# Attention, routing and 32 experts on one core: output rows by rank, experts from last to first, weights kept whole

## The chip, the cores and the metric

The kernel runs on 1 core of one Trainium2 chip. The metric is the device time in microseconds of one execution. The trace is of one profiled execution on the same kind of core.

## What is computed

A time-mixing attention over 8 batches of 128 positions and 256 channels, a residual sum, and then a mixture of experts: each of the 1024 tokens picks 4 of 32 experts, each expert takes at most 256 tokens, and a shared expert is added. All is float32. Cut to what matters:

```python
def wkv(time_decay, time_first, k, v):            # per channel, over t
    w, u = -exp(time_decay), time_first
    y_t = (exp(pp - q) * aa + exp(u + k_t - q) * v_t) / (exp(pp - q) * bb + exp(u + k_t - q))
    ...
x  = x + wkv(td, tf, layernorm(x), ctx)
z  = rmsnorm(layernorm(x)) * norm_w               # 1024 tokens x 256
scores  = softmax(z @ gate_w.T)                   # 32 experts
w, ids  = top_k(scores, 4);  w = w / sum(w)
buf[expert, position in expert] = z[token]        # 32 x 256 slots, further ones dropped
act = silu(buf @ w13[:, :128]) * (buf @ w13[:, 128:])
routed[token] += (act @ w2)[expert, position] * w
out = x + layernorm(x) + routed + (silu(z @ sg) * (z @ su)) @ sd
```

## The kernel before

**Queues.** Five engines run their own programs and meet by semaphores. SyncE (SP) issues nearly all plain transfers in the order of its program; GpSimd (POOL) issues the indirect ones, which scatter 128 rows each by a list of row numbers; ScalarE (ACT) stores three output tiles.

**Attention and routing** (`run`, lags of stages over the 8 batches). DVE, ACT and PE work a batch through scan, reciprocal, residual sum and norms to the normed rows `n_row`. For each batch DVE finds the 4 best logits (`top_logits`, `top_experts`, L632 and L636), writes the expert numbers plus one into `tags` (`expert_tags`, L640), and makes a one-hot, a mask and with TensorE's counts the slot of each pick (`slot_numbers`, L666). ACT makes the weights' exponentials per batch (`negative_max`, `pick_weights`, L450 and L454) and copies the tags beside the rows (`tag_rows`, L459). GpSimd scatters each batch's rows four times, once for each pick, into `rows_in` (`scatter`, L318), which has 1024 rows for each expert and was zeroed by 32 transfers of SyncE (L204).

**Between.** ACT takes the silu of the shared expert (L470), DVE multiplies (L675), and PE runs the shared down matmuls (L859), then eight matmuls whose result isn't used (L864), and then the experts. SyncE has issued four loads of expert weights `w13b` of 256 KB (L210) and four of `w2_all` of 1 MB (L227) after the zeroing, waits for all scatters, and loads the rows of the first four experts.

**Experts**, from 0 to 31, in this order for each engine:

- PE: transposes of the next expert's rows (`rows_to_channels`, L874), gate and up matmuls of this one (`gate_up`, L882), down matmul of the one before (`down`, L899). The slots are in two halves of 128. The second half is worked only if the expert has more than 128 rows: PE loads a flag from `big` (`value_load`) and branches. In float32 each matmul with weights stands in the trace as two records.
- ACT: `rows_to_sbuf` (copy of the next rows to `xT`, two instructions, L476), `silu` (L481).
- DVE: `picks_of_slots` (finds the output row of each slot, three small operations, L718 to L724), `gated` (product, L730), `rows_out_to_sbuf` (copy of the result to `yo`, L737).
- GpSimd: `scatter_out`, two scatters of 128 rows to `rows_out`, to the row 4 x token + pick (L333). Slots without a pick are out of bounds and write nothing.
- SyncE: `refill`: rows of the expert four ahead, weights three ahead, and one row to `last_rows` for the overflow case (L214, L210, L221).

`w13b`, the rows `xg`, `yo` and `pick_idx` are rings of four (`WB`). The first four experts are written out; the ones from 4 to 27 run in loops (`Fori`) of four experts an iteration on SyncE, ACT and DVE; on GpSimd all 32 do. In a loop a wait compares a semaphore with a number worked out from the loop's counter. PE's program is written out whole. If an expert has more than 256 picks, GpSimd mends rows under a flag.

**Tail.** When all scatters have landed, SyncE loads `G` tile by tile, each with its four picks (L265). DVE sums five tiles, weighting by `w_all` (L769). ACT weights the other three (L503) and GpSimd adds them (L372).

## Time and profile before

| | us |
|---|---|
| median of 3 runs | 234.11 |
| the runs | 232.91 to 234.96 |
| span of the profiled execution | 228.0 |
| first transpose of the experts | 82.08 |
| last scatter of output rows starts | 200.99 |

The profile gives for each engine its busy time and for each group of instructions the source line, what it writes and reads, and what its engine waited for before it. PE is TensorE's matmuls, PEld its weight loads, DVE VectorE, ACT ScalarE, POOL GpSimd, SPq SyncE issuing transfers. "issue" and "remote" are waits whose releaser the profile doesn't show.

### The profile page before, as it was taken

What the parts mean: (1) busy time and instruction counts of PE and PEld (TensorE: products, weight loads), DVE (VectorE), ACT (ScalarE), POOL (GpSimd) and SP (SyncE); (2) the same over time, 40 slices, a digit from 0 to 9 for tenths busy, and PEclk for the clock granted to TensorE, in tenths of its full rate; (3) what the DMA queues carried; (4) which work ended last, traced back from release to release, by engine and by line L of the source; (5) the groups of instructions that cost most, each with busy time, mean ns of one, the idle gap of its engine ahead of it and who ended that gap; (6) DMA issues with size and microseconds to landing.
All of it is one profiled execution on the core that took longest, in us unless ns stands there. A gap on an engine that the chain in (4) does not pass through costs nothing.

```text
span 228.0 us, 3659 instructions
## 1 busy us (share of the span) xinstructions
PE 139.5 (61%) x819; PEld 119.8 (53%) x819; DVE 120.4 (53%) x385; ACT 84.8 (37%) x254; POOL 115.6 (51%) x140
## 2 busy tenths in 40 slices
PE   1124887787774879969895948858499479200000
PEld 0112765676663559959794837837398377100000
DVE  2878999997433344555253531536237055303990
ACT  3165678566563024434214231335225032002410
POOL 6201156888877500754563736555464646632740
PEclk9999996555555799988999788999979958755555
DMA  5999999998222264775775657465665731129930
GB/s 173 334 340 340 338 339 364 365 373 301 96 99 95 95 198 134 235 204 153 218 198 176 192 161 220 136 189 158 185 172 171 232 115 52 43 69 359 385 122 23
DMA packets 40270, 46.46 MB, mean 204 GB/s; under 512 B 4585, under 2 KB 37045, under 8 KB 40252
## 3 DMA queue, kind: packets, MB, share of 16 engines
q1 hardware_dynamic: 35200, 37.30, 53.2%
q0 software_dynamic: 4608, 8.54, 10.5%
q10 hardware_dynamic: 444, 0.40, 0.5%
q8 instruction: 9, 0.15, 0.2%
q14 instruction: 9, 0.07, 0.1%
HBM read 27.95 MB, written 22.45 MB: 221 GB/s over the span
## 4 chain that ended last, share of the span: by engine, by line
PE 36%; issue 20%; SPq 19%; another core or an unknown queue 7%; DVE 7%; DMA 5%; ACT 2%; POOL 0%; POOLq 0%; ACTq 0%; DVEq 0%
PE bank L882 18%; PE bank L899 11%; SPq L204 10%; PE bank L874 8%; SPq L227 5%; DVE part L769 4%; DMA G<-rows_out 3%; DVE act_t L730 1%; ACT xT L476 1%; DMA xg<-rows_in 1%; ACT sg L481 1%; DVE res L769 1%; SPq L210 1%; DMA rows_out<-yo,pick_idx 1%
## 5 line engine op out<-in xcount | busy, mean ns | idle before, releaser
L333 POOL DMA_INDIRECT rows_out<-yo,pick_idx x64 | 62.6, 978 | 55.7 <-issue 47.8
L882 PE MATMUL bank<-xT,w13b 128*128 128x128 f32 x368 | 51.6, 294 | 8.5 <-issue 5.6
L882 PEld LDWEIGHTS bank<-xT,w13b 128*128 128x128 f32 x368 | 48.1, 208 | 11.0 <-issue 11.0
L476 ACT ACTIVATE xT<-bank,cols 128x256 f32<-128x256 f32 x64 | 26.8, 473 | 43.0 <-PE bank L874 37.0
L899 PE MATMUL bank<-w_all,act_t 128*128 128x256 f32 x92 | 29.7, 434 | 16.0 <-DVE act_t L730 14.9
L730 DVE TENSOR_TENSOR act_t<-sg,bank 128x256 f32<-128x256 f32 x32 | 13.5, 421 | 49.3 <-ACT sg L481 36.5
L318 POOL DMA_INDIRECT rows_in<-n_row,slot_all x32 | 32.5, 1015 | 10.0 <-issue 10.0
L481 ACT ACTIVATE sg<-bank 128x256 f32<-128x256 f32 x32 | 12.3, 386 | 44.6 <-PE bank L882 25.1
L899 PEld LDWEIGHTS bank<-w_all,act_t 128*128 128x128 f32 x92 | 16.5, 209 | 18.8 <-issue 17.9
L737 DVE COPY yo<-bank 128x512 f32<-128x512 f32 x32 | 22.0, 687 | 6.6 <-remote 3.3
L874 PE MATMUL bank<-ident,xg 128*128 128x128 f32 x128 | 22.0, 301 | 1.3 <-DMA xg<-rows_in 1.2
L874 PEld LDWEIGHTS bank<-ident,xg 128*128 128x128 f32 x128 | 18.0, 157 | 6.2 <-issue 2.7
L839 PE MATMUL bank<-hT,sgu 128*128 128x128 f32 x64 | 16.1, 432 | 0.0
L308 POOL TENSOR_TENSOR rs<-ve,neg_half 128x2 f32<-128x2 f32 x8 | 5.9, 736 | 17.4 <-DVE ve L624 17.3
L839 PEld LDWEIGHTS bank<-hT,sgu 128*128 128x128 f32 x64 | 14.3, 326 | 0.0
L503 ACT ACTIVATE G<-G,w_all 128x256 f32<-128x256 f32 x12 | 5.1, 496 | 17.1 <-DMA G<-rows_out 17.1
L810 PE MATMUL bank<-ident,n_row 128*128 128x128 f32 x16 | 5.3, 430 | 9.6 <-ACT n_row L431 9.6
L718 DVE SCALAR_TENSOR_TENSOR own<-xg,iota_e 128x8 f32<-128x8 f32 x32 | 7.0, 219 | 7.4 <-issue 4.4
L562 DVE TENSOR_TENSOR_SCAN S<-decay,bank 128x512 f32<-128x512 f32 x8 | 9.7, 1209 | 1.1 <-PE bank L794 1.1
L769 DVE SCALAR_TENSOR_TENSOR part<-G,w_all,base_all 128x256 f32<-128x256 f32 x5 | 3.8, 767 | 10.4 <-DMA G<-rows_out 10.4
L794 PE MATMUL bank<-ident,ek 128*128 128x128 f32 x16 | 5.1, 420 | 6.4 <-DVE ekv L556 6.3
L819 PE MATMUL bank<-gwT,hT 128*128 128x32 f32 x32 | 7.5, 374 | 1.8 <-ACT hT L444 1.8
(109 smaller groups left out, 194.3 us busy)
## 6 DMA issues: line engine op xcount, KB each, us to landing
rows_in<-zeros SPq DMA_DIRECT2D x32, 264.0 KB, 6.4
xg<-rows_in SPq DMA_DIRECT2D x32, 264.0 KB
w13b<-in_L_ffn_w_dram SPq DMA_DIRECT2D x32, 256.0 KB
w_all<-in_L_ffn_w_dram SPq DMA_DIRECT2D x4, 1024.0 KB
...
rows_out<-yo,pick_idx POOLq DMA_INDIRECT x64
...
```

The costliest lines, as they stand in the source:

```text
L204: sp.dma_start(zv[a * P:(a + 1) * P, e:e + 2, :], zeros[:, 0:2 * RW].rearrange("p (e c) -> p e c", e=2)).then_inc(zeroed[a], 16)
L318: pool.indirect_dma_start(rows_in, bass.IndirectOffsetOnAxis(ap=slot_all[:, b, k:k + 1], axis=0), n_row[:, b, :], None)\
L333: pool.indirect_dma_start(rows_out, bass.IndirectOffsetOnAxis(ap=pick_idx[:, q, a:a + 1], axis=0), yo[:, q, a, :], None, bounds_check=PICK ...
L476: act.activation(xT[:, j, h, :], FX[j][:, h, :], ACT.Copy, scale=nw[:, h:h + 1]).then_inc(s["f_x"], 1)
L481: act.activation(sg[:, j, :], FG[j][:, 0, :], ACT.Silu).then_inc(s["f_s"], 1)
L730: dve.tensor_tensor(act_t[:, j, :], sg[:, j, :], FG[j][:, 1, :], ALU.mult).then_inc(s["f_a"], 1)
L737: dve.tensor_copy(yo[:, q, :, :], FY[q % 2]).then_inc(s["f_yo"], 1)
L769: dve.scalar_tensor_tensor(out=dst, in0=G[:, b, k, :], scalar=w_all[:, b, k:k + 1], in1=src, op0=ALU.mult, op1=ALU.add)\
L839: last = nc.tensor.matmul(SGU[:, a, :], sgu[:, h, a, :], hT[:, j, h, :], start=(h == 0), stop=(h == HC - 1))
L874: last = nc.tensor.transpose(FX[q % 2][:, h, a * P:(a + 1) * P], xg[q][:, a, h * P:(h + 1) * P], ident[:, :])
L882: last = nc.tensor.matmul(FG[q % 2][:, a, cols], w13b[q][:, h, a, :], xT[:, q % 2, h, cols], start=(h == 0), stop=(h == HC - 1))
L899: return nc.tensor.matmul(FY[q % 2][:, a, :], act_t[:, q % 2, a * P:(a + 1) * P], w2_all[:, bass.ds(e, 1), :].rearrange("p o c -> p (o c)" ...
```

## The change

- **Order of picks.** `picks_in_order` copies the 4 expert numbers beside 4 negative pick numbers and takes the 8 largest: experts in falling order, then pick numbers. These lie in `n_row` itself, so the scatter carries them; `tags` and ACT's copy are gone. Rank 0 is the token's highest expert. Row numbers of the output are 1024 x rank + token, from the highest rank block down.
- **Weights.** The exponentials are made once for all batches: DVE subtracts (`expo`), ACT exponentiates before the shared silu, and `weights_in_order`, on DVE after the third expert, sums, divides and sorts them into the new order.
- **Experts run from 31 to 0**, all programs written out, waits against constants. After 29 of them every token's rank 0 has been written, after 30 rank 1, after 31 rank 2 (`settles`).
- **Weights whole in SBUF.** `w13_all` holds all experts. Five 1 MB loads of it and three of `w2_all` are issued before the row loads, the other four during the first experts. An expert's result `yo` overwrites its own `w13` weights, and `G` the weights of four finished experts. Rings of `yo` and `pick_idx` and the waits on them are gone; the rows' ring has 6 buffers. `last_rows` is stored by two transfers.
- **Halves.** A full expert runs 4 gate and up matmuls of 256 columns, not 8 of 128. The 32 flags are bits of two numbers (`bit`, `halves`), loaded once by PE.
- **Tail.** `G` is loaded rank by rank, 1 MB each with rows of 1 KB; the last rank in four pieces. DVE sums tiles 0 to 3 in place. PE sums tiles 4 to 7 in PSUM: the base through the identity, each rank through a diagonal of its weights, made by ACT in `weight_diagonal` during the experts. ACT copies and stores these. GpSimd sums nothing.

```diff
-POOL_SUMS = (1, 3, 6)
+SUMS_DVE = B // 2
+SETTLED = E - K + 1
+DIAG_FROM = 6
 FIRST = 2
 W2L = 4
+W13L = 8
+EARLY = 5
+XB = 6
+AHEAD = 2
+BITS = 16
...
+        w13_all = sb("w13_all", [P, E, HC, 2, F])
         w2_all = sb("w2_all", [P, E, C])
-        xg = [sb(f"xg{q}", [P, 2, RW]) for q in range(WB)]
-        own = sb("own", [P, WB, 2, K])
-        owned = sb("owned", [P, WB, 2])
-        pick_idx = sb("pick_idx", [P, WB, 2], I32)
+        xg = [sb(f"xg{q}", [P, 2, RW]) for q in range(XB)]
+        own = sb("own", [P, E, 2, K])
...
+        yo = [w13_all[:, e].rearrange("p h a f -> p (h a f)").rearrange("p (a c) -> p a c", a=2) for e in range(E)]
+        G = [w13_all[:, E - 4 * (k + 1):E - 4 * k].rearrange("p e h a f -> p (e h a f)").rearrange("p (b c) -> p b c", b=B)
+             for k in range(K)]
+        total = x_all
+        diag = v_all[:, :, :].rearrange("p b c -> p (b c)").rearrange("p (q r c) -> p q r c", q=B - SUMS_DVE, r=K)
...
+            def load_w13(g):
+                sp.dma_start(w13_all[:, E - (g + 1) * n:E - g * n].rearrange("p e h a f -> p (e h) (a f)"),
+                             w13[E - (g + 1) * n:E - g * n].rearrange("e (h p) f -> p (e h) f", p=P)).then_inc(w13_in[g], 16)
+
+            def load_w2(g):
+                sp.dma_start(w2_all[:, E - (g + 1) * m:E - g * m, :],
+                             w2[E - (g + 1) * m:E - g * m].rearrange("e p c -> p e c"))\
+                    .then_inc(w2_in[g], 16)
...
+            for g in range(EARLY):
+                load_w13(g)
+                if g % 2 == 0:
+                    load_w2(g // 2)
...
+            for i in range(XB):
+                load_rows(i)
+            for i in range(E):
+                if i + XB < E:
+                    sp.wait_ge(s["f_xt"], i + 1)
+                    sp.wait_ge(s["own_done"], i + 1)
+                    load_rows(i + XB)
+                if i % 2 == 0 and EARLY + i // 2 < W13L:
+                    load_w13(EARLY + i // 2)
+                    if (EARLY + i // 2) % 2 == 0:
+                        load_w2((EARLY + i // 2) // 2)
+                if i == E // 2 + 2:
+                    sp.wait_ge(s["f_yo"], E // 2)
+                    store_last(0)
+
...
+            ranked = rows_out.rearrange("(r n) c -> r n c", r=K)
+            for r in range(K):
+                sp.wait_ge(row_out[r], 32 * SETTLED if r == 0 else 32)
+                if r == 0:
+                    sp.wait_ge(s["f_yo"], E)
+                    store_last(1)
+                    sp.wait_ge(s["fixed"], fixes)
+                rows = ranked[K - 1 - r].rearrange("(h b p) c -> p h b c", h=2, p=P)
+                home = G[r].rearrange("p (h b) c -> p h b c", h=2)
+                if r < K - 1:
+                    sp.dma_start(G[r], ranked[K - 1 - r].rearrange("(b p) c -> p b c", p=P)).then_inc(gathered[r], 16)
+                else:
+                    for c in range(SUMS_DVE):
+                        sp.dma_start(home[:, :, c, :], rows[:, :, c, :]).then_inc(last_gathered[c], 16)
...
+            pool.memset(bit[:, :], 1.0).then_inc(s["bit_set"], 1)
+            for i in range(4):
+                odd = bit[:, :].rearrange("p (g o n) -> p g o n", o=2, n=1 << i)[:, :, 1, :]
+                pool.wait_ge(s["bit_set"], i + 1)
+                pool.tensor_scalar(odd, odd, float(1 << (1 << i)), None, ALU.mult).then_inc(s["bit_set"], 1)
...
-            def scatter_out(e, q):
-                pool.wait_ge(s["pick_ready"], e + 1)
-                pool.wait_ge(s["f_yo"], e + 1)
-                pool.sem_inc(s["held_pool"], 1)
+            def scatter_out(i, e):
+                pool.wait_ge(s["f_yo"], i + 1)
                 for a in range(2):
-                    pool.indirect_dma_start(rows_out, bass.IndirectOffsetOnAxis(ap=pick_idx[:, q, a:a + 1], axis=0),
-                                            yo[:, q, a, :], None, bounds_check=PICKS - 1, oob_is_err=False)\
-                        .then_inc(row_out[q], 16)
-
+                    pool.indirect_dma_start(rows_out, bass.IndirectOffsetOnAxis(ap=pick_idx[:, e, a:a + 1], axis=0),
+                                            yo[e][:, a, :], None, bounds_check=PICKS - 1, oob_is_err=False)\
+                        .then_inc(row_out[settles(i)], 16)
...
+            act.wait_ge(s["expo_done"], 1)
+            act.activation(ew[:, :, :], expo[:, :, :], ACT.Exp).then_inc(s["ew_ready"], 1)
...
+            def weight_diagonal(q):
+                b, r = SUMS_DVE + q // K, q % K
+                if q == 0:
+                    act.wait_ge(s["w_done"], 1)
+                act.activation(diag[:, q // K, r, :], ident[:, :], ACT.Copy, scale=w_all[:, b, r:r + 1])\
+                    .then_inc(s["diag_done"], 1)
...
+            for q in range(B - SUMS_DVE):
+                act.wait_ge(s["tile_summed"], q + 1)
+                act.activation(total[:, q, :], FT[q], ACT.Copy).then_inc(s["tile_ready"], 1)
+                act.wait_ge(s["tile_ready"], q + 1)
+                act.dma_start(ov[:, SUMS_DVE + q:SUMS_DVE + q + 1, :], total[:, q:q + 1, :]).then_inc(act_out_done, 16)
...
-            def expert_tags(b, j):
+                dve.max_index(idx8[:, b, :], top8[:, b, :], LG).then_inc(s["idx_done"], 1)
+
+            def picks_in_order(b, j):
                 dve.wait_ge(s["idx_done"], b + 1)
-                dve.tensor_scalar(tags[:, b, 0:K], idx8[:, j, 0:K], 1.0, None, ALU.add).then_inc(s["expert_ready"], 1)
+                if b == 0:
+                    dve.wait_ge(s["pickno_ready"], 1)
+                dve.tensor_copy(picks[:, b, 0, :], idx8[:, b, 0:K]).then_inc(s["picks_copied"], 1)
+                dve.wait_ge(s["picks_copied"], b + 1)
+                dve.max(n_row[:, b, TAG:RW], picks[:, b].rearrange("p g k -> p (g k)")).then_inc(s["expert_ready"], 1)
...
+            dve.tensor_tensor(expo[:, :, :], top8[:, :, 0:K], top8[:, :, 0:1].to_broadcast([P, B, K]), ALU.subtract)\
+                .then_inc(s["expo_done"], 1)
...
+            def weights_in_order():
+                dve.wait_ge(s["ew_ready"], 1)
+                dve.tensor_reduce(esum[:, :], ew[:, :, :], AX.X, ALU.add).then_inc(s["esum_done"], 1)
+                dve.tensor_tensor(same[:, :, :, :], n_row[:, :, TAG:TAG + K].unsqueeze(3).to_broadcast([P, B, K, K]),
+                                  picks[:, :, 0, :].unsqueeze(2).to_broadcast([P, B, K, K]), ALU.is_equal)\
+                    .then_inc(s["same_done"], 1)
+                dve.wait_ge(s["esum_done"], 1)
+                dve.reciprocal(rsum[:, :], esum[:, :]).then_inc(s["rsum_done"], 1)
+                dve.wait_ge(s["rsum_done"], 1)
+                dve.tensor_tensor(w_pick[:, :, :], ew[:, :, :], rsum[:, :].unsqueeze(2).to_broadcast([P, B, K]), ALU.mult)\
+                    .then_inc(s["w_pick_done"], 1)
+                dve.wait_ge(s["same_done"], 1)
+                dve.wait_ge(s["w_pick_done"], 1)
+                dve.tensor_tensor(same_w[:, :, :, :], same[:, :, :, :],
+                                  w_pick[:, :, :].unsqueeze(2).to_broadcast([P, B, K, K]), ALU.mult)\
+                    .then_inc(s["same_w_done"], 1)
+                dve.wait_ge(s["same_w_done"], 1)
+                dve.tensor_reduce(w_all[:, :, :], same_w[:, :, :, :], AX.X, ALU.add).then_inc(s["w_done"], 1)
...
+            for e in range(AHEAD):
+                picks_of_slots(e)
+            for e in range(E):
                 gated(e, e % 2)
                 if e:
-                    rows_out_to_sbuf(e - 1, e - 1, 0)
-            with dve.Fori(1, E // WB - 1) as i:
-                for q in range(WB):
-                    picks_of_slots(WB * i + q, q, i)
-                    gated(WB * i + q, q % 2)
-                    rows_out_to_sbuf(WB * i + q - 1, (q - 1) % WB, i - (q == 0))
-            for e in range(E - WB, E):
-                picks_of_slots(e, e % WB, e // WB)
-                gated(e, e % 2)
-                rows_out_to_sbuf(e - 1, (e - 1) % WB, (e - 1) // WB)
-            rows_out_to_sbuf(E - 1, WB - 1, E // WB - 1)
-
-
-            dve.wait_ge(s["sh_b"], B // 2)
-            dve.wait_ge(s["w_done"], 1)
-
-            mine = [b for b in range(B) if b not in POOL_SUMS]
-            for n, b in enumerate(mine):
-                dve.wait_ge(gathered[b], 16)
-                for k in range(K):
-                    src = base_all[:, b, :] if k == 0 else part[:, n % 2, k - 1, :]
-                    dst = res[:, b, :] if k == K - 1 else part[:, n % 2, k, :]
-                    if k:
-                        dve.wait_ge(s["tail_part"], (K - 1) * n + k)
-                    if b == B - 1 and k == K // 2:
-                        dve.wait_ge(gathered[B], 16)
-                    dve.scalar_tensor_tensor(out=dst, in0=G[:, b, k, :], scalar=w_all[:, b, k:k + 1], in1=src,
-                                             op0=ALU.mult, op1=ALU.add)\
-                        .then_inc(s["res_ready" if k == K - 1 else "tail_part"], 1)
+                    rows_out_to_sbuf(e - 1)
+                if e + AHEAD < E:
+                    picks_of_slots(e + AHEAD)
+                if e == 2:
+                    weights_in_order()
...
+            for r in range(K):
+                if r < K - 1:
+                    dve.wait_ge(gathered[r], 16)
+                for b in range(SUMS_DVE):
+                    if r == K - 1:
+                        dve.wait_ge(last_gathered[b], 16)
+                    if r:
+                        dve.wait_ge(s["tail_part"], (r - 1) * SUMS_DVE + b + 1)
+                    dve.scalar_tensor_tensor(out=base_all[:, b, :], in0=G[r][:, b, :], scalar=w_all[:, b, r:r + 1],
+                                             in1=base_all[:, b, :], op0=ALU.mult, op1=ALU.add)\
+                        .then_inc(s["res_ready" if r == K - 1 else "tail_part"], 1)
...
-            def gate_up_half(q, a, cols):
-                for h in range(HC):
-                    last = nc.tensor.matmul(FG[q % 2][:, a, cols], w13b[q][:, h, a, :], xT[:, q % 2, h, cols],
-                                            start=(h == 0), stop=(h == HC - 1))
-                return last
-
-            def gate_up(e, q, n, second):
-                pe.wait_ge(w_in[q], 16 * (n + 1))
-                pe.wait_ge(s["f_x"], 2 * e + 2)
-                if not isinstance(e, int) or e >= 2:
-                    pe.wait_ge(s["f_a"], e - 1)
+            def gate_up_slots(e, j, slots):
+                for a in range(2):
+                    for h in range(HC):
+                        last = nc.tensor.matmul(FG[j][:, a, 0:slots], w13_all[:, expert(e), h, a, :], xT[:, j, h, 0:slots],
+                                                start=(h == 0), stop=(h == HC - 1))
+                last.then_inc(s["f_g"], 1)
...
+            flags = [pe.value_load(big[0:1, g:g + 1], min_val=0, max_val=(1 << BITS) - 1) for g in range(E // BITS)]
+
+            def second(e):
+                return flags[expert(e) // BITS] & (1 << expert(e) % BITS)
...
+            pe.wait_ge(s["sh_b"], B // 2)
+            pe.wait_ge(s["diag_done"], (B - SUMS_DVE) * K)
+            for q in range(B - SUMS_DVE):
+                nc.tensor.matmul(FT[q], ident[:, :], base_all[:, SUMS_DVE + q, :], start=True, stop=False)
+            for r in range(K):
+                if r < K - 1:
+                    pe.wait_ge(gathered[r], 16)
+                for q in range(B - SUMS_DVE):
+                    if r == K - 1:
+                        pe.wait_ge(last_gathered[q], 16)
+                    last = nc.tensor.matmul(FT[q], diag[:, q, r, :], G[r][:, SUMS_DVE + q, :], start=False,
+                                            stop=(r == K - 1))
+                    if r == K - 1:
+                        last.then_inc(s["tile_summed"], 1)
```

## Rows read from the trace of the kernel before

**Rows 1.** Table by stages: stretch, length; PE, PEld, DVE, ACT, POOL busy; clock; DMA; GB/s.

```profile
20.00:30.00 10.00, 7.31 (x32) 5.95 (x32) 9.22 (x31) 7.85 (x27) 0.70 (x1) 1.00 1.10 339
82.00:198.20 116.20, 90.75 (x588) 80.18 (x588) 49.01 (x161) 37.28 (x96) 60.03 (x62) 0.90 0.57 168
198.20:228.00 29.80, 0.00 (x0) 0.00 (x0) 13.45 (x20) 5.12 (x12) 11.74 (x15) 0.50 0.51 187
```

**Rows 2.** Timeline before the experts: start, length, engine, line, what, idle before.

```profile
31.48 1.31 POOL L318 DMA_INDIRECT rows_in<-n_row,slot_all  x1 [0.28 <-issue]
...
33.94 11.90 SPq L227 DMA_DIRECT2D w_all<-in_L_ffn_w_dram  x4
...
76.65 0.96 POOL L318 DMA_INDIRECT rows_in<-n_row,slot_all  x1 [0.30 <-issue]
```

**Rows 3.** Chain that ended last, first experts: start, us, what.

```profile
86.35 1.79 PE bank L882 x16
88.14 0.87 PE bank L899 x4
89.00 0.44 PE bank L874 x4
...
94.72 0.89 PE bank L882 x8
```

**Rows 4.** Groups of instructions: busy us, mean ns, idle before.

```profile
L899 PE MATMUL bank<-w_all,act_t 128*128 128x256 f32 x92 | 29.7, 434 | 16.0 <-DVE act_t L730 14.9 <-issue 1.2
```

**Rows 5.** Timeline in the experts.

```profile
90.64 1.20 POOL L333 DMA_INDIRECT rows_out<-yo,pick_idx  x1 [6.95 <-DVE pick_idx L724]
...
157.46 1.13 PE L882 MATMUL bank<-xT,w13b 128*128 128x128 f32 x8
...
159.39 0.98 POOL L333 DMA_INDIRECT rows_out<-yo,pick_idx  x1 [0.30 <-issue]
...
160.67 0.97 POOL L333 DMA_INDIRECT rows_out<-yo,pick_idx  x1 [0.30 <-issue]
...
161.59 0.23 DVE L718 SCALAR_TENSOR_TENSOR own<-xg,iota_e 128x8 f32<-128x8 f32 x1 [3.36 <-issue]
...
164.02 0.00 SPq L214 DMA_DIRECT2D xg<-rows_in  x1
...
164.11 0.39 ACT L481 ACTIVATE sg<-bank 128x256 f32<-128x256 f32 x1 [4.90 <-remote]
```

**Rows 6.** Waits: engine, line, releaser: us in total, times, longest.

```profile
ACT sg L481 <- remote: 18.2, 5, 5.7
```

**Rows 7.** Timeline of the last expert and the tail.

```profile
194.87 0.38 ACT L481 ACTIVATE sg<-bank 128x256 f32<-128x256 f32 x1 [3.28 <-remote]
...
203.44 4.89 SPq L265 DMA_DIRECT2D G<-rows_out  x9
206.78 0.48 DVE L769 SCALAR_TENSOR_TENSOR part<-G,w_all,base_all 128x256 f32<-128x256 f32 x1 [8.58 <-DMA G<-rows_out]
...
222.11 0.48 DVE L769 SCALAR_TENSOR_TENSOR res<-G,w_all,part 128x256 f32<-128x256 f32 x1
```

**Rows 8.** The same chain at the last scatter.

```profile
200.99 2.30 DMA rows_out<-yo,pick_idx
```

**Rows 9.** Timeline of the shared expert and the first transposes.

```profile
68.10 1.28 ACT L470 ACT_TABLE_LOAD   x1
69.39 1.06 ACT L470 ACTIVATE sg_all<-gu_all 128x1024 f32<-128x1024 f32 x1
70.02 0.29 DVE L666 TENSOR_REDUCE slot_all<-picked 128x4 int32<-128x128 f32 x1
70.48 1.23 DVE L675 TENSOR_TENSOR sg_all<-sg_all,gu_all 128x1024 f32<-128x1024 f32 x1 [0.17 <-issue]
...
82.08 1.30 PE L874 MATMUL bank<-ident,xg 128*128 128x128 f32 x8 [1.19 <-DMA xg<-rows_in]
```

**Rows 10.** DMA traffic in GB/s in 40 slices of 5.7 us.

```profile
GB/s 173 334 340 340 338 339 364 365 373 301 96 99 95 95 198 134 235 204 153 218 198 176 192 161 220 136 189 158 185 172 171 232 115 52 43 69 359 385 122 23
```

311 lines of the change are left out of this document (118 added, 193 removed).

## The prediction, made before the changed kernel was run

> **What bounds the kernel now.** I read the table by stages first [rows 1]: attention and routing up to 82 us, the 32 experts from 82 to 198.2 us, then the tail to 228.0 us. No engine is full in the experts: TensorE 0.78 of the time, GpSimd 0.52.
>
> In the first part GpSimd issues 32 scatters of input rows, from 31.48 to 76.65, one each 1.46 us, and the last comes with no wait but its issue [rows 2]. That stream sets the end.
>
> In the experts the chain of work gives TensorE's price [rows 3]. A full expert (over 128 slots) takes 0.44 + 1.79 + 0.87 = 3.10 us (86.35 on), a half one 0.44 + 0.89 + 0.43 (half of the 0.87) = 1.76. The down matmuls are 92 records, two per matmul [rows 4]: 46 matmuls for 32 experts, so 14 are full. TensorE needs 14 x 3.10 + 18 x 1.76 = 75.1 us of the 116.1 us (82.1 to 198.2); 41.0 are lost. GpSimd's output scatters come 1.28 us apart [rows 5]: 64 x 1.28 = 81.9, also less than 116.1.
>
> Where the 41 us lie is the main point. In [rows 5] an expert's up matmuls start at 157.46 and take 1.13 us, but ScalarE's silu of them starts at 164.11, after 4.90 us idle put down to "remote". SyncE's row load of 164.02 comes at that moment too, although the VectorE work it waits for ended at 161.82. So signals come late, on several engines at once. The waits [rows 6] hold 18.2 us of this on the silu line alone. In this stage SyncE, ScalarE, VectorE and GpSimd run in loops (`Fori`) and wait against computed numbers. While three of them were still in written-out code, TensorE ran without a gap [rows 3]. But the last silu, written out too, idles 3.28 us on "remote" [rows 7], so loops may not be the whole cause.
>
> The tail: the last scatter starts at 200.99 and lands 2.30 later [rows 8], SyncE starts the `G` loads at 203.44, VectorE's last sum ends at 222.6, and 5.4 us of output and closing follow [rows 7].
>
> **The change, part by part.** The profiled span is 228.0 us and the median of the runs 234.11; I keep the 6.1 between them.
>
> *Start.* `picks_in_order` puts a COPY and a MAX8 where one TENSOR_SCALAR stood. At this size I bound both by 0.29 from above (the 0.29 of [rows 9] works on 128 columns) and by nothing from below, and take 0.2 more a batch. VectorE is full there (9.22 of 10 us [rows 1]), for two batches before GpSimd's stream is closed: +0.4, scatters end at about 78. Four ScalarE operations a batch go; ScalarE had room (7.85 of 10), so nothing is gained. Five small operations for `bit` go to GpSimd when it is nearly idle (0.70 of 10). SyncE issues eight 1 MB loads ahead of the row loads where it had four and four small ones. Four took 11.90 us, so from 33.94 eight take it to 58 [rows 2]; its next work is at 78. The 3 MB more fill 9 us of the DMA after 57 us, where it moves only 96 GB/s [rows 10].
>
> ScalarE's Exp and the silu behind it now wait for `expo`, and so for VectorE's last slot numbers. These end at 70.31; + 0.2 (subtract) + 0.3 (Exp) + 1.28 + 1.06 (table, silu) + 1.23 makes 74.6 for `sg_all`, where it was 71.71 [rows 9]. The shared matmuls, the warming ones and the first transposes follow in TensorE's order. TensorE waited 1.19 us for the row loads [rows 9], which covers 1.1 of these 2.9: +1.8, the first transpose at 83.9. The flags' `value_load`, now two ahead of the experts, is not shown: 0 to 0.5, hidden by the warming matmuls.
>
> *Experts.* Full experts run four up matmuls of 256 columns, eight records at 0.87/4 = 1.73, not 1.79: TensorE 14 x 3.04 + 18 x 1.76 = 74.3. Waits on rings go, and nothing is queued behind GpSimd, since `yo` lies in each expert's own weights. VectorE works 49.0/32 = 1.53 us an expert [rows 1], under 1.76. `weights_in_order`, seven operations of 0.2 to 0.3, adds 1.5 once; the 16 diagonals are at most 0.39 each on ScalarE (the silu of twice the columns [rows 5]), which works 37.3/32 = 1.2 an expert. GpSimd's stream hides all of it: 81.9 against 74.3. Without that cover the 1.5 costs 1.5. The order turned round puts a full expert first and a half one second, 0.9 better for the first `yo`, + 1.8: the first scatter goes from 90.64 [rows 5] to 91.5, the last starts 63 x 1.28 later, at 172.1, against 200.99.
>
> *Tail.* The first rank waits for 29 experts: 172.1 - 7.7 + 2.3 = 166.7, then `store_last`, 0.3. It also waits for the last `yo`, which TensorE leaves at about 160. 512 KB land 3.3 us after the issue (203.44 to 206.78) and as much again at 385 GB/s [rows 10] takes 1.4: some 4.6 for 1 MB, then one each 2.6 to 3.1 us; I take 2.9. Ranks land at 171.6, 174.5, 177.4, the four pieces of the last (issued 174.5 to 176.3) by 180.3. VectorE adds four tiles a rank at 0.48 (the rate at 222.11), hidden. TensorE does four matmuls a rank, two records each: 0.43 a matmul at the higher clock, 0.86 at the lower, and it starts at the lower, as the tail of before shows 0.50 [rows 1]. All low it ends at 185.3, all high at 180.7. It had come up during the shared matmuls; I take 181.0. Copy 0.5, handing over 0.4, then 5.4: 187.3.
>
> A word on run length. Rank loads move 1 KB runs where 4 KB were read. The slices show 338 to 373 GB/s with 1 KB runs at the start, 359 and 385 in the tail [rows 10]; hence the 2.6 to 3.1. The Trainium skill ("Perfetto Trace Analysis", DMA Optimizations) says that DMAs under 2 KB have a significant overhead each. It gives no figure to put in the sum; the slices here show under a tenth.
>
> *Sum.* Last scatter 28.9 earlier, tail 27.0 to 15.2: 228.0 - 28.9 - 11.8 = 187.3; + 6.1 = 193.4. I say 194.
>
> **The rivals.** *Half the lateness stays (204 us).* Part of the 41.0 us isn't the loops': TensorE ends at 83.9 + 74.3 + 20.5 = 178.7, the last scatter starts 2.8 later (198.2 to 200.99 before), 9.4 after the forecast's; one more for less overlap. For it: the last silu. The Trainium skill ("Advanced Engine Details and Errata", ISA Cache) says that an engine other than TensorE holds 32 KB of instructions, 512 of them, so written-out loops must be fetched as they run. No row here shows a wait for that.
>
> *All of it stays (226 us).* It belongs to the output scatters, not the loops. TensorE ends at 83.9 + 74.3 + 41.0 = 199.2; rank loads start only then, the first lands at 204.2, the last at 212.9; + 7.0 + 6.1 = 226.0. For it: the stall of [rows 5] lasts as long as GpSimd issues. Against it: GpSimd streamed from 31 to 78 us too, and the others kept its pace.
>
> *Slower (261 us).* The same mechanism, but GpSimd is no longer held to four experts, streams without end, and TensorE's signals pass only when it rests. They take turns: 83.9 + 74.3 + 81.9 = 240.1, + 15 + 6. It decides from 49 us of lateness on, against 41.0 now. Against it: GpSimd issued for 82 us, and half of that was lost.
>
> **How the numbers follow.** Forecast 0.50, half 0.24, all 0.19, slower 0.04, something within 1% 0.03. A measurement of this kernel can't tell 1% from no change. Faster: 0.93. The floor is 194 less the start's 1.8, less 1.2 (2.6 a rank) and some 2 us of the 6.1 and the tail: 189; I go to 188. The upper end takes in the half case and half of the next: 222. The forecast's own range is 188 to 199, with the slow TensorE tail at its top.
>
> **What would show it.** Right: output scatters 1.28 us apart without gaps, TensorE's experts done some 8 to 10 us before GpSimd's, silus within 0.5 us of their matmuls, first transpose near 83.9, ranks landing 2.6 to 3.1 us apart. Wrong: GpSimd idle between experts, "remote" waits on the silu line, or rank loads that begin only after the last scatter. The forecast fails most easily at the 41 us, which I give to the loops on thin evidence.

## The result, and the profile after

| | before | after |
|---|---|---|
| median, 5 runs each | 232.91 us | 218.10 us |
| the runs | 232.23 to 234.96 | 215.86 to 218.78 |
| ratio | | 0.936 (0.930 to 0.942) |
| span of the profiled execution | 228.0 | 214.1 |
| first transpose of the experts | 82.08 | 90.89 |
| TensorE's last down matmul ends | 197.46 | 191.19 |
| last output scatter starts | 200.99 | 196.75 |

Faster, by 14.8 us where I forecast 40. The 13.9 us between the spans are made up of a loss of 8.8 at the start, a gain of 15.1 in the experts (115.4 to 100.3 on TensorE) and one of 7.6 behind TensorE's last down matmul (30.5 to 22.9).

The start first. GpSimd's timeline of the changed kernel (start, length, engine, line, what, idle before):

```profile
2.08 0.10 POOL L305 MEMSET var_add<- 128x1 f32 x1
11.31 0.16 POOL L306 IOTA iota_e<- 128x32 f32 x1 [9.13 <-issue]
...
40.38 1.31 POOL L342 DMA_INDIRECT rows_in<-n_row,slot_all  x1 [0.21 <-issue]
...
84.74 0.96 POOL L342 DMA_INDIRECT rows_in<-n_row,slot_all  x1 [0.30 <-issue]
```

GpSimd stands still for 9.13 us before its first index tile, waiting for nothing that the profile shows. In the kernel before, the input scatters ran from 31.48 to 76.65 [rows 2]; here all of them are 8 to 9 us later. I had nothing of this in the sum.

The experts, timeline and waits of the changed kernel:

```profile
90.89 1.04 PE L870 MATMUL bank<-ident,xg 128*128 128x128 f32 x8
...
98.58 1.20 POOL L355 DMA_INDIRECT rows_out<-w_all,pick_idx  x1 [6.51 <-DVE w_all L744]
...
103.44 1.06 PE L879 MATMUL bank<-xT,w_all 128*128 128x128 f32 x8
...
105.97 1.06 PE L879 MATMUL bank<-xT,w_all 128*128 128x128 f32 x8
...
107.77 0.97 POOL L355 DMA_INDIRECT rows_out<-w_all,pick_idx  x1 [0.30 <-issue]
109.36 0.38 ACT L477 ACTIVATE sg<-bank 128x256 f32<-128x256 f32 x1 [4.17 <-remote]
110.11 0.68 DVE L744 COPY w_all<-bank 128x512 f32<-128x512 f32 x1
...
111.57 0.97 POOL L355 DMA_INDIRECT rows_out<-w_all,pick_idx  x1 [2.83 <-DVE w_all L744]
```

```profile
POOL rows_out L355 <- DVE w_all L744: 24.3, 12, 6.5
...
ACT sg L477 <- remote: 12.9, 9, 4.2
```

This is the picture of [rows 5] again, with every loop gone. The up matmuls of 103.44 end at 104.50, and TensorE is already at the next expert's at 105.97, but ScalarE's silu of the first ones starts only at 109.36, after 4.17 us of waiting. GpSimd issues eight scatters back to back until 108.74; the silu starts 0.6 us behind them. Then the result comes, and GpSimd has run dry and waits in its turn: 24.3 us in all. It isn't so everywhere. From 117 to 139 us, where GpSimd rests about 0.7 us between experts, TensorE is busy for 19.7 of 22 us.

Table by stages of the changed kernel (stretch, length; PE, PEld, DVE, ACT, POOL busy; clock; DMA; GB/s), the experts and what follows:

```profile
90.90:191.20 100.30, 85.34 (x478) 72.67 (x477) 49.25 (x167) 43.16 (x112) 57.87 (x60) 0.93 0.52 160
191.20:214.10 22.90, 12.66 (x40) 8.07 (x39) 7.65 (x17) 1.53 (x4) 4.99 (x6) 0.84 0.79 250
```

The tail, same timeline, SyncE, VectorE and GpSimd:

```profile
192.55 8.40 SPq L284 DMA_DIRECT2D w_all<-rows_out  x3
...
196.75 0.97 POOL L355 DMA_INDIRECT rows_out<-w_all,pick_idx  x1 [0.30 <-issue]
198.71 1.67 DVE L767 SCALAR_TENSOR_TENSOR base_all<-w_all,base_all 128x256 f32<-128x256 f32 x4 [6.79 <-DMA w_all<-rows_out]
...
202.67 1.90 SPq L287 DMA_DIRECT2D w_all<-rows_out  x4
202.71 1.67 DVE L767 SCALAR_TENSOR_TENSOR base_all<-w_all,base_all 128x256 f32<-128x256 f32 x4 [2.33 <-DMA w_all<-rows_out]
...
206.30 1.67 DVE L767 SCALAR_TENSOR_TENSOR base_all<-w_all,base_all 128x256 f32<-128x256 f32 x4 [1.91 <-DMA w_all<-rows_out]
```

The first rank's load goes out at 192.55, before the last scatter starts, as the order by rank was meant to allow. Ranks arrive at 198.7, 202.7 and 206.3. But the scatters land late. The last one needs 5.9 us, where it needed 2.30 before [rows 8], and the last rank's load goes out only at 202.67. Two loads of 1 MB (192.55 and 194.38) were issued ahead of it, a third at 200.59. The chain of work that ended last runs through the scatter of 194.19, which needs 6.38 us, and the third rank's load behind it:

```profile
194.19 6.38 DMA rows_out<-w_all,pick_idx
200.57 0.02 issue
200.59 5.69 DMA w_all<-rows_out
```

### The profile page after: what moved, and what is told of

Read it like the earlier page. It is cut to its first block, busy times and chain, and to the rows that moved or that the text cites. A ratio compares the mean times of both kernels' runs of the same rounds, so it can differ in the third digit from the quotient of the medians.

```text
span 214.1 us, 2773 instructions
## 1 busy us (share of the span) xinstructions
PE 145.6 (68%) x747; PEld 119.6 (56%) x747; DVE 115.7 (54%) x396; ACT 83.8 (39%) x231; POOL 106.8 (50%) x133
## 4 chain that ended last, share of the span: by engine, by line
PE 34%; issue 21%; POOL 13%; DVE 10%; ACT 9%; DMA 6%; another core or an unknown queue 5%; ACTq 1%; POOLq 0%; DVEq 0%
PE bank L879 14%; POOL rows_in L342 9%; PE bank L893 7%; PE bank L870 7%; ACT xT L472 4%; DMA rows_out<-w_all,pick_idx 3%; PE bank L857 3%; DMA w_all<-rows_out 3%; DVE S L554 2%; POOL rs L333 2%; PE bank L928 1%; ACT sg L477 1%; DVE act_t L740 1%; DVE st L513 1%
## 5 line engine op out<-in xcount | busy, mean ns | idle before, releaser
L355 POOL DMA_INDIRECT rows_out<-w_all,pick_idx x64 | 62.5, 976 | 43.2 <-DVE w_all L744 24.3
L879 PE MATMUL bank<-xT,w_all 128*128 128x128 f32 (+1 forms) x256 | 50.4, 343 | 5.6 <-ACT xT L472 3.4
L879 PEld LDWEIGHTS bank<-xT,w_all 128*128 128x128 f32 x256 | 40.7, 204 | 10.6 <-issue 7.6
L740 DVE TENSOR_TENSOR act_t<-sg,bank 128x256 f32<-128x256 f32 x32 | 13.4, 420 | 42.9 <-ACT sg L477 29.5
L893 PE MATMUL bank<-w_all,act_t 128*128 128x256 f32 x92 | 27.2, 405 | 9.4 <-DVE act_t L740 5.7
L477 ACT ACTIVATE sg<-bank 128x256 f32<-128x256 f32 x32 | 12.3, 383 | 33.5 <-PE bank L879 17.9
L744 DVE COPY w_all<-bank 128x512 f32<-128x512 f32 x32 | 21.9, 685 | 4.6 <-PE bank L893 2.7
L928 PE MATMUL bank<-w_all,v_all 128*128 128x256 f32 x32 | 10.9, 481 | 7.3 <-DMA w_all<-rows_out 7.2
L333 POOL TENSOR_TENSOR rs<-ve,neg_half 128x2 f32<-128x2 f32 x8 | 5.7, 714 | 17.9 <-DVE ve L616 17.7
L767 DVE SCALAR_TENSOR_TENSOR base_all<-w_all,base_all 128x256 f32<-128x256 f32 x16 | 7.0, 481 | 12.0 <-DMA w_all<-rows_out 12.0
L928 PEld LDWEIGHTS bank<-w_all,v_all 128*128 128x128 f32 x32 | 6.9, 236 | 11.3 <-DMA w_all<-rows_out 10.4
L800 PE MATMUL bank<-ident,Y 128*128 128x128 f32 x16 | 5.3, 429 | 10.7 <-DVE Y L591 6.9
L800 PEld LDWEIGHTS bank<-ident,Y 128*128 128x128 f32 x16 | 2.2, 196 | 13.7 <-DVE Y L591 8.3
```

The costliest lines, as they stand in the source:

```text
L355: pool.indirect_dma_start(rows_out, bass.IndirectOffsetOnAxis(ap=pick_idx[:, e, a:a + 1], axis=0), yo[e][:, a, :], None, bounds_check=PICK ...
L477: act.activation(sg[:, j, :], FG[j][:, 0, :], ACT.Silu).then_inc(s["f_s"], 1)
L740: dve.tensor_tensor(act_t[:, j, :], sg[:, j, :], FG[j][:, 1, :], ALU.mult).then_inc(s["f_a"], 1)
L744: dve.tensor_copy(yo[expert(e)], FY[e % 2]).then_inc(s["f_yo"], 1)
L879: last = nc.tensor.matmul(FG[j][:, a, 0:slots], w13_all[:, expert(e), h, a, :], xT[:, j, h, 0:slots], start=(h == 0), stop=(h == HC - 1))
L893: return nc.tensor.matmul(FY[j][:, a, :], act_t[:, j, a * P:(a + 1) * P], w2_all[:, expert(e), :], start=True, stop=True)
```

## The experiments

Sixteen runs in four sets, each set on a chip of its own, with the kernel before timed beside it. That kernel took 206.3 and 206.9 us beside the first two sets, and 237.4 and 237.2 beside the last two, where it had taken 232.9 beside the result. So the chips differ, by more than the change is worth. I call the first two *prompt* and the last two, with the result's, *late*, for a reason that the traces give below. Only numbers of one kind are compared. No two sets share a chip, so whether it is the chip itself or what else went on around it is not shown. scatters_after, before_again, quiet_experts, dry_scatters and after_third are one execution each; what they show is read from their traces, stage by stage.

### First set (prompt): the start, the scatters, the loops

**scatters_after.** GpSimd is silent while TensorE works on the experts:

```diff
+            pool.wait_ge(s["f_yo"], E)
             for i in range(E):
                 scatter_out(i, expert(i))
```

and at the start `pool.memset(idle[:, 0], 0.0)` and the same for `idle[:, 1]`, two tiles of 256 columns, stand before `ident`'s memset.

> The changed kernel with two edits that lie far apart. At the start GpSimd sets two more small tiles (2 x 0.3 us) before its first index tile, so that it comes there no earlier than in the kernel before (2.8 us instead of 2.2). Theory S1: the 9.1 us for which GpSimd stands still there (2.2 to 11.3) depend on the moment at which it arrives, and are gone or much shorter. Theory S2: they come from something the program holds further on, and stay at 8 to 9 us. In the experts GpSimd waits until all 32 results are written before it issues the first output scatter, so that it is silent while TensorE works. Theory E1 (signals pass late while GpSimd issues scatters): the experts take TensorE 74.3 us plus at most 3, that is 75 to 78 us from the first transpose to the last down matmul, where the changed kernel took 100.1, and the silus follow their matmuls within 0.5 us. Theory E2 (the lateness belongs to transfers of rows and weights or to the fetching of instructions): 92 to 100 us as now. The whole is slower by either, since 64 x 1.28 = 82 us of scatters follow: about 165 + 82 + 17 = 264 us of span by E1 and 290 by E2, 9 less if the start's wait goes.

270.0 us. GpSimd's first index tile comes at 14.56 after 11.88 us of waiting, so arriving later doesn't help: S1 is out. The experts took 76.0 us, as E1 said. But this chip couldn't answer, as the next run showed.

**bits_later.** The five operations on `bit` stand behind the first `rstd1`, otherwise the changed kernel.

> The changed kernel with one edit: the five small operations that make the powers of two stand behind the first scales, out of the chain of the start. Theory S2c: they are what makes GpSimd stand still for 9.1 us before its first index tile; the wait goes and the whole gains 9 us. Otherwise the wait stays, and the first transpose is earlier by the 1.4 us that the five operations take between 12.20 and 13.72: 216.5 instead of 218.1.

197.46 us (195.45 to 199.50), with the kernel before at 206.27. The wait stays (9.37 us), S2c is out. With all 64 scatters in place the last down matmul ends at 164.49, 76.2 us behind the first transpose (88.28). Here the changed kernel has no lateness at all.

**skip_empty.** For an empty half, 16 rows are scattered instead of 128; `picks` is float32.

```diff
+                half(0)
+                with pool.If((full[e // BITS] & (1 << e % BITS)) != 0):
+                    half(1)
+                with pool.Else():
+                    pool.indirect_dma_start(rows_out, bass.IndirectOffsetOnAxis(ap=pick_idx[0:16, e, 1:2], axis=0), ...)
```

> The changed kernel with two edits. At the start the tile of pick numbers is float32 instead of int32 (GpSimd's third index tile). Theory S2a: an int32 index tile is what makes GpSimd stand still for 9.1 us before its first one, and that goes. S1 and S2b (another part of the program): it stays. In the experts GpSimd reads the two numbers of flags too, and for the 18 experts that fill only one half it scatters 16 rows in place of 128 empty ones. A scatter costs 1.28 us whatever it holds or less with fewer rows; the row shows which. Theory E1 (GpSimd's issuing holds back TensorE's signals, and GpSimd and TensorE take turns): each microsecond of scattering saved is saved in the end: if a scatter of 16 rows costs 0.5 us, 18 x 0.8 = 14 us, a ratio near 0.94 to this kernel's 218.1; at 1.28 each nothing. Theory E2 (lateness has another cause): TensorE loses the same 26 us, its last down matmul stays at 191, and the whole within 1% (plus or minus the start's 9).

196.41 us, ratio to before 0.955 (0.943 to 0.967). The wait at the start is 10.44 us: no S2a either. GpSimd's timeline in this kernel, the scatters of 16 rows at L363 among those of 128:

```profile
162.50 0.86 POOL L363 DMA_INDIRECT rows_out<-w_all,pick_idx  x1 [0.30 <-issue]
163.66 0.98 POOL L356 DMA_INDIRECT rows_out<-w_all,pick_idx  x1 [0.30 <-issue]
```

A scatter of an eighth of the rows costs 1.16 us against 1.28. Nearly the whole price is for issuing one. First to last scatter took 78.8 us, where 64 full ones take 80.7; 18 x 0.12 = 2.2 us were to be expected, and 1.9 are measured. To save, a scatter must be left out.

**before_no_loops.** The kernel before, each `with engine.Fori(1, E // WB - 1) as i:` made `for i in range(1, E // WB - 1):` (GpSimd's from 0).

> The kernel before with one edit: the loops of SyncE, ScalarE, VectorE and GpSimd are written out, so that every wait is against a constant. Theory L (the one the prediction rests on): the loops hold back the engines, TensorE's experts fall from 116 us towards 82 (GpSimd's 64 scatters), and the whole by 25 to 34 us, to about 200 to 207. Theory E1 (GpSimd's issuing holds back TensorE's signals): the loops have little part, the experts take 105 to 116 us, the whole 222 to 233. Start: the 9.1 us of GpSimd at the first index tile do not appear if they come from the new operations; if they come from the length of the programs, they appear here too.

204.95 us, ratio to before 0.996 (0.991 to 1.001), experts 89.4 us. No gain in the whole. GpSimd's index tile waits 0.29 us with the programs written out, so their length isn't the cause of the start's wait. On a prompt chip, though, there was little lateness for the loops to be blamed for. So the question stayed open for a late chip.

### Second set (prompt): which kind of chip, and the cause of the start's wait

Between the traces of before and after one difference was left at GpSimd's start. The trace has a pair of configuration instructions (MODIFY_POOL_CONFIG) before each change of the kind of its work. Before has three pairs: at 2.8, after the input scatters (ahead of `slot_top`'s reduction over partitions) and at 202.0, ahead of the sums. After has two: it sums nothing on GpSimd, and ends with what the reduction needed.

**before_again**, **after_again**: both kernels unchanged.

> The kernel before, unchanged, for a profile on this chip. Theory C (the lateness of signals belongs to the chip or its core, not to the kernel): on a chip where it takes about 206 us, the experts take near 92 us from the first transpose to the last scatter's start minus 3, against 116 us in the first profile, and the silu line has hardly any wait put down to remote (18.2 us before). Theory K (it belongs to the kernel): 18 us of remote here too.

> The changed kernel, unchanged. Theory C: on a chip where before takes 206 us it takes 196 to 199 us; its scatters run 1.28 us apart without gaps, 80.6 us from the first to the last, where the first profile had 98.2. Theory K: 215 to 218 again. In either case GpSimd stands still for 9 to 12 us before its first index tile.

207.18, and 198.88 us with a ratio of 0.965 (0.959 to 0.971) to before. Tables by stages of the experts, before_again and then after_again:

```profile
82.20:172.90 90.70, 82.07 (x588) 72.88 (x588) 49.02 (x161) 39.17 (x96) 58.41 (x61) 0.98 0.74 214
```

```profile
90.10:166.60 76.50, 75.42 (x477) 67.57 (x478) 50.63 (x167) 43.61 (x112) 53.03 (x55) 1.00 0.68 210
```

No wait of either is put down to "remote". TensorE is full after the change. Before it, another wait is at work. The waits of before_again, and then the same row in the first profile of the kernel before:

```profile
DVE own L718 <- DMA rows_out<-yo,pick_idx: 22.9, 18, 3.2
...
DVE own L718 <- DMA rows_out<-yo,pick_idx: 3.0, 2, 2.4
```

VectorE waits 18 times for the ring of four (`yo`, `pick_idx`) to come free. In before_again the chain of work that ended last passes eight times through a scatter on which the ring waits, 31.5 us in all; in the experts of the first profile it never does. One of the eight:

```profile
120.38 3.67 DMA rows_out<-yo,pick_idx
```

The experts shrink by 90.6 - 76.5 = 14.1 us, and I put this down to the ring. It is an upper bound: no run took away the ring alone, 1.2 us may be the loops' (89.4 us in before_no_loops), and the wider matmuls and the earlier loads have a part too. GpSimd's scatters run as forecast in after_again: 80.7 us from first to last.

**library_back.** One edit:

```diff
             for i in range(E):
                 scatter_out(i, expert(i))
+            pool.iota(spare[:, :], [[1, E]], base=0, channel_multiplier=0, ...)
```

> The changed kernel with one edit: after its last output scatter GpSimd makes one small index tile that nobody reads. Theory S3: GpSimd's reduction over partitions uses other code than index tiles and sums do (the profile has a pair of configuration instructions before each change of kind), the changed kernel ends with the former loaded because GpSimd sums nothing in its tail, and so the next execution must load the latter again, 9 to 12 us at its start. With the index tile at the end the loading moves into the tail, where GpSimd is idle for 15 us: the wait before the first index tile goes to 0.3 us, everything after it is 9 us earlier, ratio to the unchanged kernel about 0.95. If S3 is wrong the wait stays and the time is the same.

193.59 us, ratio to before 0.936 (0.931 to 0.941). GpSimd's timeline in this kernel:

```profile
2.47 0.16 POOL L307 IOTA iota_e<- 128x32 f32 x1 [0.28 <-issue]
...
185.11 0.16 POOL L367 IOTA spare<- 128x32 f32 x1 [10.48 <-issue]
```

S3 holds. The wait has moved from the first index tile to the last one, where it costs nothing. What a program ends with decides whether its *next* execution pays the wait. That the wait is the loading of GpSimd's code for the new kind of work is the reading that fits; the trace doesn't show the loading itself. The first transpose is at 82.10, 8.0 us earlier than in after_again, and as early as before. The time fell by only 5.3. Where did the rest go? The tables by stages over the first 10 us of the experts, library_back and then after_again:

```profile
82.00:92.00 10.00, 9.29 (x41) 7.82 (x42) 3.19 (x15) 3.51 (x9) 0.38 (x1) 0.66 0.98 306
```

```profile
90.00:100.00 10.00, 9.31 (x64) 8.24 (x65) 5.48 (x25) 5.62 (x14) 2.28 (x3) 1.00 0.97 312
```

TensorE had the lower clock (1.2 GHz) in part of the first stretch (0.50 from 85 to 88 us) and did 41 matmuls in the time of 64. The first scatter is 5.0 us earlier (92.77 against 97.79), not 8.0, and the last 4.9.

**combined.** library_back and bits_later together, and no scatter at all for an empty half. The numbers that SyncE waits for (16 for each scatter of a rank) are worked out by VectorE from the counts, and loaded into registers:

```diff
+                half(0)
+                with pool.If((full[e // BITS] & (1 << e % BITS)) != 0):
+                    half(1)
...
+            dues = [sp.value_load(due[0:1, r:r + 1], min_val=16, max_val=1024) for r in range(K)]
...
-                sp.wait_ge(row_out[r], 32 * SETTLED if r == 0 else 32)
+                sp.wait_ge(row_out[r], dues[r] if r == 0 else dues[K - r])
```

> The changed kernel with three edits: the index tile at the end as in the run beside it, the five operations for the powers of two behind the first scales, and no scatter at all for the empty halves of 18 experts (GpSimd branches on the flags; the numbers that SyncE waits for before it loads the ranks are worked out from them). By the theory that GpSimd's 64 scatters set the end wherever signals come in time, its 46 scatters (59 us) no longer do, TensorE's 74.3 us do: the last scatter starts 3 to 4 us after TensorE's last down matmul, the first rank load 5 us earlier than in the run beside it, and the whole is 5 to 7 us below it and about 15 us below the changed kernel, near 182 us where the kernel before takes 206. If the ranks' loads set the end instead, it gains only what the first of them starts earlier.

182.76 us, ratio to before 0.883 (0.878 to 0.889): 16.1 us below the changed kernel, as expected, and 10.8 below library_back, where 5 to 7 were. Its timeline at the end of the experts:

```profile
159.90 0.97 POOL L361 DMA_INDIRECT rows_out<-w_all,pick_idx  x1 [0.34 <-issue]
...
161.04 7.00 SPq L290 DMA_DIRECT2D w_all<-rows_out  x3
...
163.73 0.97 POOL L361 DMA_INDIRECT rows_out<-w_all,pick_idx  x1 [0.30 <-issue]
...
169.81 2.15 SPq L293 DMA_DIRECT2D w_all<-rows_out  x4
```

TensorE's last down matmul ends at 159.69 and the last scatter starts 4.0 us later, where it was 12.0 in after_again. TensorE is now the bound. The last scatter again takes 6.1 us to land, and this trace shows since when: the scatters of 158.59 and 159.90 land after 2.1 and 2.5 us, the one of 161.18, the first behind a rank's load (161.04), after 6.5. In scatters_after the last thirteen scatters up to 244.80 land after 2.1 to 2.4 us, and the next, which starts 0.1 us ahead of the first rank's load (246.16), after 5.3.

### Third set (late): is it GpSimd?

**after_control**: the changed kernel unchanged.

> The changed kernel, unchanged, beside the other runs of this set. Theory C (late signals belong to the chip): if the kernel before takes about 206 us here, this takes 196 to 201 and shows no more than 1 us of waits put down to remote on the silu line; if the kernel before takes about 233 us, this takes 215 to 219 and shows 10 us or more.

226.15 us beside 237.43, ratio 0.943 (0.932 to 0.954); 17 us of "remote" on ScalarE's two lines (8.9 on the copy of the rows, 8.2 on the silu, where 10 were expected). The time is above the 215 to 219 expected too. On the chips of the third and fourth set the changed kernel also reaches its experts later, at 94.1 to 96.6 us instead of 90.9 beside the result, with GpSimd silent in the experts or not. That isn't explained, and stages alone are compared here.

**quiet_experts**: `pool.wait_ge(s["f_yo"], E)` ahead of the output scatters, alone.

> The changed kernel with GpSimd waiting for all 32 results before its first output scatter. Theory E1 (where signals come late, they do so while GpSimd issues scatters back to back) is only tested on a chip where the kernel before takes about 233 us: there the experts, which took 100.1 us in the first profile, fall to 75 to 79. If they stay above 90, GpSimd's scatters are not what holds the signals back. On a chip where before takes 206 the run repeats an earlier one: about 77 us.

271.1 us in all. What counts is the stage. Tables by stages of the experts on the same chip, after_control and then quiet_experts:

```profile
96.60:202.10 105.50, 85.92 (x478) 73.21 (x477) 49.52 (x165) 42.58 (x112) 58.12 (x60) 0.92 0.48 145
```

```profile
94.10:170.10 76.00, 74.96 (x478) 67.64 (x477) 49.34 (x168) 43.67 (x112) 0.00 (x0) 1.00 0.51 150
```

With GpSimd silent the experts take 76.0 us on the late chip, as on the prompt one, and no wait on ScalarE is put down to "remote". The rows, the weights, the instructions that are fetched are the same. So the late signals in the experts come with GpSimd's scatters, and only on this kind of chip. The two rows also show in what the 29.5 us consist. TensorE's busy time is 11.0 us longer with the scatters, at a granted clock of 0.92 instead of 1.00: after its pauses it works at the lower clock for a while. Beside the result it is busy for 2.5 of 6 us from 105 to 111 us, and its clock is 0.72 from 111 to 117. The other 18.5 us it is idle.

**long_runs.** Row 8 x partition + batch within a rank instead of 128 x batch + partition, so that a partition reads 8 KB in one piece:

```diff
-            pool.iota(picks[:, :, 1, :], [[T, B], [B * T, K]], base=-OUTSIDE, channel_multiplier=1)
+            pool.iota(picks[:, :, 1, :], [[1, B], [B * T, K]], base=-OUTSIDE, channel_multiplier=B)
...
-                    sp.dma_start(G[r], ranked[K - 1 - r].rearrange("(b p) c -> p b c", p=P))
+                    sp.dma_start(G[r], ranked[K - 1 - r].rearrange("(p b) c -> p b c", p=P))
```

> The changed kernel with the rows of a rank stored in another order (row 8 x partition + batch instead of 128 x batch + partition), so that the loads of ranks 0 to 2 move runs of 8 KB to each partition instead of 1 KB; the last rank's pieces stay at 1 KB. Theory R (short runs make the ranks' loads slow; 1 MB took 3.6 to 4.9 us where I forecast 2.9): ranks 1 and 2 come at 2.7 to 3.0 us each, and the end 3 to 4 us earlier, ratio to the control 0.98. Theory Q (the loads share the DMA with the last scatters, and the run's length is not what counts): ranks within 0.3 us of the control's, the time the same within 0.5%. The scatters write single rows of 1 KB in both.

219.46 us, ratio to before 0.926 (0.919 to 0.933), against the control's 0.943: 0.98 of it, the size that R gave, but not all where R said. From the first rank's load to the last sums of rank 2, it took 11.6 us against 13.7; another 3.3 lie in the experts (102.2 against 105.5 us), which the order of the rows has no reason to shorten. Ranks came 2.9 and 3.1 us apart against 3.2 and 4.0. But with short runs combined has 3.0 and 3.0 and after_third, on a late chip, 3.7 and 3.3, while combined_long has 3.3 and 3.3. R is not shown. What the ranks' distance does follow stays open.

**combined_long**: combined and long_runs together.

> The combined kernel (index tile at the end, powers of two later, no scatter for empty halves) with the order of rows of the long-run kernel. By R about 179 us where combined took 182.8 beside 206.9; by Q the same 182 to 183. On a chip with late signals it tells what the whole is worth there: the start gives 5 to 9 us, and 18 scatters fewer give more than elsewhere if they hold back TensorE (E1): 233 down to 190 to 198; otherwise about 205.

195.95 us, ratio to before 0.827 (0.819 to 0.834). The experts take 84.2 us with 46 scatters, where 64 of them made it 102.2 to 105.5.

### Fourth set (late): loops, data or issue

**no_loops_again**: before_no_loops once more.

> The kernel before with its loops written out, again, since its first run was on a chip that shows no late signals. On a chip where the kernel before takes about 233 us: theory L (loops and computed waits cause or enlarge the lateness): experts well under 115 us and the whole under 225. Theory E1 (GpSimd's scatters alone): experts 110 to 118 and the whole within 2% of before. On a chip where before takes 206: the same as before, which tells nothing new.

234.14 us with the kernel before at 237.16. Its experts take 115.8 us (87.4 to 203.2); those of before took 115.4 in the first profile (no trace of before was taken on this chip). Theory L, which wanted them well under 115 and the whole under 225, falls on the late chip too. Whether the loops are worth the 1% between the two times these runs can't tell. Its waits:

```profile
ACT sg L481 <- remote: 15.3, 4, 5.0
```

**dry_scatters.** The 64 real scatters stand behind the experts, and in their old places as many whose row numbers (`far`, from 16384 on) are all out of bounds. They write no rows.

```diff
+            for i in range(E):
+                pool.wait_ge(s["f_yo"], i + 1)
+                for a in range(2):
+                    pool.indirect_dma_start(rows_out, bass.IndirectOffsetOnAxis(ap=far[:, a:a + 1], axis=0), ...)
```

> The changed kernel with its 64 output scatters moved behind the experts, and in their old places 64 scatters of the same size whose row numbers all lie out of bounds, so that they move no data. Where signals come late (before takes about 233): theory D (it is the data that the scatters write, 8.5 MB in single rows): the experts fall to 76 us as with a silent GpSimd. Theory I (it is GpSimd's issuing itself): they stay at 95 to 105. On a chip without lateness 76 to 78 in either case.

**after_third**: the changed kernel unchanged.

> The changed kernel, unchanged, as the measure for the run with scatters that move nothing: experts 100 to 106 us on a chip with late signals, 76 to 77 on one without; GpSimd's wait before its first index tile 9 to 12 us on either.

306.4 and 222.8 us. Tables by stages of the experts, dry_scatters and then after_third:

```profile
95.90:201.70 105.80, 85.49 (x478) 73.21 (x477) 49.36 (x167) 42.57 (x112) 58.87 (x61) 0.92 0.41 114
```

```profile
96.20:198.70 102.50, 85.72 (x478) 73.65 (x477) 49.71 (x167) 42.92 (x112) 57.52 (x59) 0.92 0.49 148
```

DMA queue of GpSimd's scatters in the experts (packets, MB, share), dry_scatters and then after_third:

```profile
q0 software_dynamic: 2880, 0.03, 1.8%
...
q0 software_dynamic: 2784, 3.79, 11.1%
```

The scatters hold back the signals just as well when they write no rows: 0.03 MB against 3.79. So it isn't the data but their issue, with the small packets that go with it, which these runs don't tell apart. The timeline of dry_scatters shows a case. TensorE's transposes of 108.06 are done at 108.66, and ScalarE copies them at 112.33:

```profile
108.06 0.60 PE L880 MATMUL bank<-ident,xg 128*128 128x128 f32 x4
...
111.55 0.97 POOL L371 DMA_INDIRECT rows_out<-w_all,far  x1 [0.31 <-issue]
112.33 0.84 ACT L482 ACTIVATE xT<-bank,cols 128x256 f32<-128x256 f32 x2 [3.92 <-PE bank L880]
112.83 0.97 POOL L371 DMA_INDIRECT rows_out<-w_all,far  x1 [0.30 <-issue]
...
115.22 0.38 ACT L487 ACTIVATE sg<-bank 128x256 f32<-128x256 f32 x1 [2.04 <-remote]
```

**combined_again**: combined, short runs.

> The combined kernel (index tile at the end, powers of two later, no scatter for empty halves), with short runs in the ranks. On a chip where before takes about 233: 194 to 200 as the one with long runs did (195.95 beside 237.4), since the run's length was worth 2 to 3% at most there. On a chip where before takes 206: 181 to 184.

196.12 us, ratio to before 0.838 (0.822 to 0.854), experts 85.0 us. Long runs gave 195.95 in the other late set, beside a before within 0.3 us: the run's length is worth nothing that these runs show.

## Why the prediction was wrong

The sum said 187.3 us of span and it was 214.1. Three terms make up the 26.8: 7.1 in the first output scatter (98.58, not 91.5), 17.5 in gaps of GpSimd's stream (98.2 us for 63 intervals, not 80.6), 2.2 in the tail (17.4 behind the last scatter's start, not 15.2). The step that failed is the one that gave the 41 us to the loops and so let GpSimd's stream set the end without gaps. That 218.1 us lies within the range of 188 to 222 is no merit of it: the range reached there for the sake of the rivals, and 7 us come from a term that no case had.

**The start: a term was missing.** "+1.8, the first transpose at 83.9"; it came at 90.9, 8.8 later than before. The missing term is GpSimd's wait of 9.13 us before its first index tile. library_back moves it away and brings the first transpose from 90.07 to 82.10. It could have been suspected: the tail's sums on GpSimd were on my list of removed work, and I asked what removing them frees, not what the engine is left with. And the trace of before had a row with such a wait, ahead of the reduction:

```profile
83.31 0.38 POOL L326 PARTITION_ALL_REDUCE slot_top<-slot_max  x1 [5.70 <-issue]
```

Of the 1.8 itself nothing is seen: library_back's first transpose is at 82.10, before_again's at 82.21. Both wait for the row loads (1.62 and 2.93 us), and the later `sg_all` hides in that. (Its terms add up to 74.4, not 74.6.)

**The experts: the 41 us were given to the wrong cause.** "the 41 us, which I give to the loops on thin evidence": without loops the experts take 115.8 us on a late chip, as before. The 38.9 above the 76.5 that TensorE needs are two other things. Up to 14.1 belong to the ring of four (by the prompt chips; that they add up on the late one is an estimate), and 24.8 are left, which go with GpSimd's issuing. The change took away the first and kept the second: 100.3 - 76.5 = 23.8. Of these, 9.9 are TensorE's own busy time (85.3 us against 75.4), at a clock of 0.93 against 1.00. My step "Waits on rings go" was right and had no price: the trace of before shows 3.0 us for this wait, where results that came late anyway left little to wait for.

The evidence against the loops was in hand. The last silu, written out, idled 3.28 us on "remote" [rows 7], and in [rows 5] the stall lasted as long as GpSimd issued. I set against it that GpSimd had streamed from 31 to 78 us too, where "the others kept its pace". On late chips that isn't so either: in this stretch VectorE has 3.8 us of "remote" on the line of the slots even in quiet_experts, and it had 2.3 in the trace of before.

**The rivals.** "It belongs to the output scatters, not the loops" had the cause right, and its size wrong (226, 41 us kept): it gave the scatters the ring's share. "Half the lateness stays" had about the size (204, 20.5 us kept, and 26.0 were), but by luck: no half of it was the loops'. With the 7.0 us by which the first transpose came late it would have been 211. The slower rival's mechanism, engines that take turns, is what the timeline shows at its worst; its price was too high, since GpSimd runs dry by itself after two to eight scatters, and then the signals pass. Its "49 us of lateness" I can't work out from the rows given.

**What held.** On the prompt chips the forecast's experts are there: TensorE 76.5 us (74.3 forecast), 80.7 us of scatters at 1.28 us without a gap, the last scatter 12.0 us behind TensorE's end (13.9). The full gate and up matmuls take 1.73 us, as worked out from the 0.87. after_again's span of 196.4 is 9.1 above the forecast's 187.3, but that it equals the missing wait is chance: the last scatter starts 6.4 late (178.53, not 172.1) and the tail is 2.7 longer (17.9, not 15.2), and without the wait library_back's span is still 193.4. A full expert's matmuls in the chain of work of the changed kernel (start, us, what):

```profile
115.92 1.73 PE bank L879 x8
```

**The tail.** "The first rank waits for 29 experts" was right. The landing of the last scatters was mis-sized: 6.4 and 5.9 us, not 2.3, and 5.9 and 6.1 for the last one in after_again and combined. The loads put ahead of them are the cause by their place in time: within one trace the landing goes from 2.1 to 2.5 us to over 5 with the first of them, in combined and in scatters_after. No run held them back. Ranks came 4.0 and 3.6 us apart, not 2.9. Of the Trainium skill's rule on DMAs under 2 KB ("Perfetto Trace Analysis", DMA Optimizations) the runs with 8 KB pieces show no effect in the whole (195.95 against 196.12 us).

**Around the span.** I kept 6.1 us between span and median. Each run's own span lies 1.8 below its time. The other 4.3 came from comparing one quick execution with the median of others; for the changed kernel too the profiled one is the fastest of five. From 187.3 + 6.1 = 193.4: + 26.8 - 6.1 + 1.8 + 2.2 (the median run against the profiled) = 218.1.

What stays open: what in the issue of a scatter keeps other engines' signals back, why one kind of chip shows it and another doesn't, and what the ring costs by itself.
